# Layer norm statistics of the scan and FFN stage on ScalarE and GpSimd instead of VectorE

## The reference

```
def _layernorm(x, axis=-1, eps=1e-05):
    m = jnp.mean(x, axis=axis, keepdims=True)
    v = jnp.var(x, axis=axis, keepdims=True)
    return (x - m) / jnp.sqrt(v + eps)

x = x + ffn(_layernorm(x))      # x = fwht(x * SU_ug); silu(x @ Wg.T) * (x @ Wu.T); fwht; x @ Wd.T
x = x + ssm(ctx, _layernorm(x)) # the second argument is the gate z:
    state = state * exp(d_t * A) + (d_t * u_t) * B_t ; y_t = state . C_t
    y = (y + D * u) * silu(z)
```

## Time and profile before

| what | value |
|---|---|
| median of three runs | 2714.7 us |
| the profiled execution, its own time | 2715.96 us |
| its span | 2714.2 us |
| granted TensorE clock, mean | 0.917 |
| busy over the span: PE, DVE, POOL, ACT | 85%, 69%, 50%, 45% |
| scan, L1862 DVE, 256 times | mean 1222 ns |
| product, L1873 DVE, 180 times; sum, L1879 DVE, 60 times | mean 691 ns |
| inner, L1887 DVE; add_y, L1893 DVE, 64 times each | mean 750 and 683 ns |
| decay, L1693 ACT, 256 times | mean 692 ns |

### The profile page before, as it was taken

The page is one execution under the profiler, slowest core; times in us unless marked ns, Lnnn a source line. Parts: engine busy times, 40 slices in busy tenths (PEclk is TensorE's granted clock), DMA queues, the critical chain, the costliest instruction groups (busy, mean ns, idle before and its releaser), DMA issues. The chain is left out here.

```text
span 2714.2 us, 35174 instructions
## 1 busy us (share of the span) xinstructions
PE 2294.5 (85%) x10784; PEld 1768.1 (65%) x10785; DVE 1860.2 (69%) x3465; ACT 1229.2 (45%) x2129; POOL 1350.1 (50%) x1083
## 2 busy tenths in 40 slices
PE   3799999999999999997856997998988749468980
PEld 2688888888888888885525665665655427356770
DVE  6476777777676767765757999999989766312223
ACT  2354445445444545443655655656555312123430
POOL 0233333333333333331756778988888602577324
PEclk7799999999999999998977999999999958779995
DMA  7522232221223232112467564654554220755317
GB/s 280 218 75 79 86 110 86 109 87 72 82 86 110 86 110 85 63 67 81 139 219 216 177 205 144 213 175 172 180 195 156 61 90 16 250 164 183 120 54 259
DMA packets 136907, 363.57 MB, mean 134 GB/s; under 512 B 21281, under 2 KB 58913, under 8 KB 118561
## 3 DMA queue, kind: packets, MB, share of 16 engines
q1 hardware_dynamic: 123648, 328.36, 35.6%
q0 software_dynamic: 6320, 20.71, 2.4%
q10 hardware_dynamic: 6768, 12.32, 1.2%
HBM read 290.06 MB, written 71.30 MB: 133 GB/s over the span
## 5 line engine op out<-in xcount | busy, mean ns | idle before, releaser
L664 POOL TENSOR_SCALAR att_probs<-att_probs,att_recip 128x512 f32<-128x512 f32 x256 | 181.7, 713 | 563.1 <-DVE att_recip L731 563.1
L1809 POOL TENSOR_TENSOR mix_drive<-mix_du,mix_rows 128x512 f32<-128x512 f32 x256 | 326.6, 1282 | 63.2 <-DMA mix_rows<-bc_d 28.9
L588 ACT ACTIVATE att_probs<-att_s,att_bias,att_rq 128x512 f32<-128x512 f32 x256 | 200.4, 783 | 289.7 <-DVE att_bias L727 289.6
L1862 DVE TENSOR_TENSOR_SCAN mix_state<-mix_state,mix_drive 128x512 f32<-128x512 f32 x256 | 312.8, 1222 | 15.5 <-POOL mix_drive L1809 10.5
L1693 ACT ACTIVATE mix_state<-mix_delta,mix_a 128x512 f32<-128x512 f32 x256 | 176.7, 692 | 276.9 <-DVE mix_drive L1873 237.7
L1794 POOL TENSOR_TENSOR mix_y<-mix_y,mix_drive 128x512 f32<-128x512 f32 x180 | 230.4, 1280 | 78.2 <-DVE mix_drive L1873 78.2
L1602 PE MATMUL mix_down<-mix_wd,mix_hT 128*128 128x512 f32 x512 | 233.9, 600 | 7.5 <-DVE residual_x L1893 7.5
L726 DVE TENSOR_REDUCE att_nmax<-att_s 128x1 f32<-128x512 f32 x256 | 175.2, 684 | 71.7 <-PE att_s L101 64.8
L767 DVE TENSOR_TENSOR att_pT<-att_pt,att_pT 128x512 fp32r<-128x512 f32 x256 | 170.1, 686 | 65.0 <-ACT att_pT L594 61.3
L594 ACT CAST att_pT<-att_pt 128x512 fp32r<-128x512 f32 x256 | 144.0, 592 | 132.8 <-PE att_pt L445 128.5
L99 PE MATMUL att_w<-att_w_qkv,att_cx 128*128 128x256 f32 x512 | 158.6, 310 | 34.2 <-DVE att_w_qkv L713 25.5
(11 more groups left out here) (348 smaller groups left out, 6718.4 us busy)
## 6 DMA issues: line engine op xcount, KB each, us to landing
att_xn<-normT SPq DMA_DIRECT2D x32, 2048.0 KB
mix_gu<-guT SPq DMA_DIRECT2D x64, 1024.0 KB
mix_rows<-bc_d SPq DMA_DIRECT2D x128, 256.0 KB, 5.0
guT<-att_ffnT SPq DMA_DIRECT2D x32, 512.0 KB, 5.7
mix_wd<-wdT SPq DMA_DIRECT2D x16, 1024.0 KB
slots<-exp_y ACTq DMA_DIRECT2D x47, 256.0 KB
normT<-nrm_outT SPq DMA_DIRECT2D x4, 2048.0 KB, 9.3
exp_raw<-in_L_ffn_Wg SPq DMA_DIRECT2D x16, 512.0 KB
```

Of the source, the lines that this page charges most:

```text
L588: act.activation(probs[:, n, :], ps_s[n % 2][:, :], ACT.Exp, bias=bias[:, n:n + 1], scale=rq[:, n:n + 1], accum_out=sums[:, n:n + 1]).then ...
L664: pool.tensor_scalar(probs[:, n, :], probs[:, n, :], recip[:, n:n + 1], 1.0, ALU.mult, ALU.mult).then_inc(s_pn, 1)
L1809: pool.tensor_tensor(drive[q % RING][:, :], du[i % DUS][:, :], rows[g % ROWS][:, 0, :], ALU.mult).then_inc(s_drive, 1)
L1862: dve.tensor_tensor_scan(h[:, :], h[:, :], drive[q % RING][:, :], 0.0, ALU.mult, ALU.add).then_inc(s_scan, 1)
```

## The change

The statistics leave DVE. For each row tile ACT now runs an Identity pass with an accumulated sum, a multiplication by -1/512 on 128x1, and a Square pass with minus the mean as bias and an accumulated sum (`moments`). `stats(b, j)` does this for one or two row tiles at the end of ACT's steps j = 0 to 3; the passes write their elementwise output into `normT`, which is not read then. Three semaphores make each of the three kinds wait for the one before. POOL makes `rstd` with a power of -0.5 and `shift` (`spread`), three small instructions in its step j = 5, behind its first product there. DVE's list loses `normal_stats`, `gate_stats` and `spread`, and nothing is added to it. In the tail ACT takes the last four row tiles one by one as they are summed, POOL does `spread` behind the last `skip_add`, and the gate follows.

```diff
+                summed, centred, squared = Steps(act, s_sums), Steps(act, s_minus), Steps(act, s_squares)
+
+                def moments(tiles):
+                    squared.wait()
+                    for c, row in tiles:
+                        summed.mark(act.activation(normT[:, c // TB, :], xs[:, row, :], ACT.Identity,
+                                                   accum_out=sums[:, c:c + 1]))
+                    summed.wait()
+                    for c, row in tiles:
+                        centred.mark(act.mul(minus[:, c:c + 1], sums[:, c:c + 1], -1.0 / DIM))
+                    centred.wait()
+                    for c, row in tiles:
+                        squared.mark(act.activation(normT[:, c // TB, :], xs[:, row, :], ACT.Square, bias=minus[:, c:c + 1],
+                                                    accum_out=squares[:, c:c + 1]))
+
+                def stats(b, t):
+                    tiles = []
+                    if b + 1 < B:
+                        tiles.append((t, (b + 1) * TB + t))
+                    if b:
+                        act.wait_ge(s_yadd, BLOCKS * (b - 1) + (CHUNK - 1) * TB + t + 1)
+                        tiles.append((TB + t, (b - 1) * TB + t))
+                        if t == 0:
+                            act.wait_ge(s_rot, KD * min(b, B - 1))
+                    moments(tiles)
 ...
@@ -1759,6 +1786,10 @@
                     if s + 1 < ALL:
                         decay(q + 2)
                         decay(q + 3)
+                    if j < TB:
+                        stats(b, j)
+                    if j == TB:
+                        squared.wait()
 ...
                 for t in range(TB):
+                    stats(B, t)
+                for t in range(TB):
                     z(B - 1, t)
 ...
+                def spread(b, done):
+                    c = slice(0 if b + 1 < B else TB, 2 * TB if b else TB)
+                    if b and b + 1 < B:
+                        pool.wait_ge(s_nrm, TB * b)
+                    if b >= 2:
+                        pool.wait_ge(s_z, TB * (b - 1))
+                    pool.wait_ge(s_squares, done)
+                    pool.tensor_scalar(var_eps[:, c], squares[:, c], 1.0 / DIM, LN_EPS, ALU.mult, ALU.add).then_inc(s_var, 1)
+                    pool.wait_ge(s_var, b + 1)
+                    pool.tensor_tensor(rstd[:, c], var_eps[:, c], power[:, c], ALU.pow).then_inc(s_root, 1)
+                    pool.wait_ge(s_root, b + 1)
+                    pool.tensor_tensor(shift[:, c], minus[:, c], rstd[:, c], ALU.mult).then_inc(s_rs, 1)
+
+                def moments_made(b):
+                    return TB * (b + 1) + TB * b - (TB if b >= B - 1 else 0) - (TB if b == B else 0)
+
+                pool.memset(power[:, :], -0.5).then_inc(s_power, 1)
                 for q in range(RING):
                     force(q)
                 pool.wait_ge(s_const, 64)
+                pool.wait_ge(s_power, 1)
                 for s in range(ALL):
                     b, j = divmod(s, BLOCKS)
                     for q in range(ET * (s + 1), ET * (s + 2)):
                         add(q - RING)
                         if s + 1 < ALL:
                             force(q)
+                        if j == TB + 1 and q % ET == 0:
+                            spread(b, moments_made(b))
 ...
                     skip_add(B - 1, t)
+                spread(B, moments_made(B))
 ...
-                def normal_stats(b, t):
-                    own.mark(dve.bn_stats(stats[:, t, :], xs[:, b * TB + t, :]))
-
-                def gate_stats(b, t):
-                    dve.wait_ge(s_yadd, BLOCKS * b + (CHUNK - 1) * TB + t + 1)
-                    own.mark(dve.bn_stats(stats[:, TB + t, :], xs[:, b * TB + t, :]))
-
-                def spread(first, last):
-                    c = slice(first, last)
-                    own.wait()
-                    for t in range(first, last):
-                        own.mark(dve.bn_aggr(meanvar[:, t, :], stats[:, t, :]))
-                    own.wait()
-                    own.after(dve.tensor_scalar(var_eps[:, c], meanvar[:, c, 1], LN_EPS, None, ALU.add))
-                    newton_rsqrt(dve, own, rstd[:, c], var_eps[:, c], guess[:, c], newton[:, c])
-                    dve.scalar_tensor_tensor(shift[:, c], meanvar[:, c, 0], -1.0, rstd[:, c], ALU.mult,
-                                             ALU.mult).then_inc(s_rs, 1)
-
                 def rotated_lo(b, o):
                     dve.wait_ge(s_rhi, KD * (b - 1) + o + 1)
                     dve.scalar_tensor_tensor(uT[b % 2][:, 1, o, :], spare[o % 2][:, :], SC,
@@ -1945,17 +1979,6 @@
                     if s + 1 < ALL:
                         scan(q + 1)
                         scan(q + 2)
-                    if j < TB:
-                        if b + 1 < B:
-                            normal_stats(b + 1, j)
-                        if b:
-                            gate_stats(b - 1, j)
-                    if j == TB:
-                        if b and b + 1 < B:
-                            dve.wait_ge(s_nrm, TB * b)
-                        if b >= 2:
-                            dve.wait_ge(s_z, TB * (b - 1))
-                        spread(0 if b + 1 < B else TB, 2 * TB if b else TB)
                     if b + 1 < B:
                         if j == 8:
                             rotated_lo(b + 1, 0)
@@ -1976,9 +1999,6 @@
                         scan(q + 3)
                 for n in range(ALL - LAG - 1, ALL):
                     add_y(n)
-                    gate_stats(B - 1, n % TB)
-                dve.wait_ge(s_z, TB * (B - 1))
-                spread(TB, 2 * TB)
                 for t in range(ET):
                     gated(B - 1, t)
                 for t in range(TB):
```

More of the change, by code:

```diff
@@ L1436, in stage_mix @@
         d = m.sb("skip", [P, ET])
[L1437 to L1438 removed]
+        sums = m.sb("sums", [P, 2 * TB])
+        minus = m.sb("minus_mean", [P, 2 * TB])
+        squares = m.sb("squares", [P, 2 * TB])
         var_eps = m.sb("var_eps", [P, 2 * TB])
[L1440 to L1441 removed]
+        power = m.sb("power", [P, 2 * TB])
         rstd = m.sb("rstd", [P, 2 * TB])
```

8 lines of the change are left out of this document (2 added, 6 removed).

## The result

The changed kernel took 2683.44 us (median of 4 runs, 2679.82 to 2687.01), the kernel before 2713.65 (median of 4, 2711.42 to 2715.6): ratio 0.9889, 95% interval 0.9873 to 0.9905. 2695 was predicted, with a range from 2686 to 2712. The direction was right. The profiled execution took 2687.01, its span is 2685.1.

What follows compares the result with a forecast made beforehand. DVE was taken as full, setting the ordinary step at 9.77 us, with POOL next. Terms 2.4 + 6.0 + 8.8 + 5.8 - 1.3 - 0.1 = 21.6 off 2715.96 gave 2694.4, rounded up to 2695; range 2686 to 2712.

Steps and rivals of the forecast that it cites:

- Batch 0, j = 0 to 3: First four steps of batch 0: without the statistic DVE needs 9.16 a step instead of 9.76, 2.4 us saved.
- Batch 0, j = 4: Batch 0's spread step: POOL's spread and ACT's passes are covered, the step falls to 9.76, 6.0 us saved.
- Batches 1 and 2, j = 0 to 3: Steps with two statistics: POOL's unbroken list keeps them at 11.7 each, so nothing is saved.
- Batches 1 and 2, j = 4: Spread steps: ACT's norm waits for POOL, inner comes at 1681.6 instead of 1686.04, 4.4 us saved twice, 8.8.
- Batch 3: Nothing at j = 0 to 3; 8.3 saved at j = 4, of which 1.5 and 1.0 come back: 5.8 us.
- PE: Before the rotations: with less pause from DVE's spreads PE comes later, 1.3 us lost, bounds nothing and 3.7.
- the rival that PE takes the gain back: Each batch's gain at j = 4 only moves the wait to the rotations, some 20 us go: 2713, 7%.
- The tail: After the last add_y: ACT takes 2.1 and POOL 2.4, ending at 2166.5 instead of 2166.39, 0.1 us lost.
- ACT's block: ACT's new statistics work between two decays: 2.1 us for one row tile, 4.1 for two, upper bound 4.6.
- the slower rival: Long hand-overs make ACT's two-tile work 7.6 us: 2725, slower than before from about 6.7, 9%.
- POOL's spread: Inverse root and shift on POOL: power 1.73, two small instructions 0.3 each, 2.4 us in all, bounds 1.8 and 5.3.
- the first rival: POOL's small instructions are dear, the spread takes up to 5.3, each us paid five times: gain 7, 2709, 17%.

Runs made afterwards that it cites:

- the repeat: The changed kernel timed and profiled once more with nothing altered: 2687.05 us, ratio 0.9897 to the kernel before.
- skip_half: Changed kernel with skip_add divided, multiplication on DVE and addition on POOL, and u loads issued earlier: 2675.44 us, ratio 0.9859 to the kernel before.
- half_split: skip_half with ACT's new work cut in two around the fourth decay of a step: 2675.62 us, ratio 0.9843 to the kernel before.

## Why the prediction was wrong

By its steps, with the first profile and the repeat:

- **Batch 0, j = 0 to 3:** 2.4 predicted, 2.39 measured, steps of 9.17. Right.
- **Batch 0, j = 4:** 6.0 predicted, 5.69 and 6.01. Right.
- **Batches 1 and 2, j = 0 to 3:** nothing predicted, 3.2 and 3.7 measured. This is the step that failed. What held is that POOL sets these steps: without the late loads they are equal to 0.1 us with and without the statistics, and they fall when POOL is relieved. What failed is the sentence that POOL "works through" from 1624.52 to 1674.18 and that, nothing being removed from its list, the product comes no earlier. The earlier trace rows has only the two ends of that list. Inside it lie waits for the loads of u, 3.9 us with batch 3, which I had not looked for, and these depend on DVE's steps by way of SyncE's queue. With the statistics gone 0.5 or nothing is left of them.
- **Batches 1 and 2, j = 4:** 8.8 predicted, 9.15 and 9.10. `norm` waits for POOL as described. The step is 13.5 where 13.6 was said.
- **Batch 3:** 5.8 predicted, 6.86 and 6.88. 8.0 came at j = 4 and 0.2 ahead of it, and 1.3 went back in the rest where 2.5 was booked.
- **PE:** a loss of 1.3 predicted. In the first profile the rest of batch 0 is 1.2 longer, in the repeat 0.3 shorter: it is 115.1 in four profiles with the whole change in them and 113.7 in five (in skip_half and half_split j = 15 has new work of its own). What decides between the two is open. The rests of batches 1 and 2 are shorter by 0.3 together. So the term was a loss of 0.9 in the first profile and a gain of 0.5 in the repeat. DVE's waits for PE's down product in the steps are 11.9 and 10.4 where they were 11.1, and the rival that PE takes the gain back is out.
- **The tail:** a loss of 0.1 predicted, 0.8 gained. ACT's block for one tile is 1.8 there and POOL's spread on 128x4 is 1.6, where 2.1 and 2.4 were put.
- **ACT's block:** 4.1 predicted, 3.1 measured. The 7.3 of the path around it was right to 0.05. The error cost nothing in the sum, since POOL's list lay above both, but the cover was 0.8 to 0.9 a step (11.2 against 10.36) and not 0.3, and the even point of the slower rival is 7.1 and not 6.7.
- **POOL's spread:** 2.4 predicted, 2.2 from 1671.88 to the next sum at 1674.07. Its small instructions took 0.20, so the first rival is out, and each us of the spread is paid nearly five times, as was said. The Trainium skill (SBUF — State Buffer, "SBUF: two separate sides") names a DVE instruction with two SBUF inputs or in a two-port mode as one that takes the shared port pair. DVE's scans and products have one input in PSUM, and the 0.20 of POOL beside them agree.

The stage sum is thus 27.2 or 29.4 where 21.6 stood: 3.3 to 3.9 from the loads, 0.9 from the tail, 0.9 from batch 3 besides its load, and the remainder of 0.5 to 2.1 mostly from PE's term. The medians say 30.2, which the stage of the first profile alone does not explain. That the other 1 to 3 us are run-to-run variation outside the stage follows from the repeat (ratio 0.9897) only within its interval of 0.15%. One step of the working had its sign wrong: the prediction rounded up because the profiled execution was 1.3 above the median. That speaks for rounding down: from the median the sum gives 2714.7 - 21.6 = 2693.1, not 2695. With the 3.3 to 3.9 of the loads that would have been some 2689 to 2690, inside the range.

## What to carry over

An engine's list of rows without idle time has to be looked through for small waits before it is called fixed: here 3.9 us of POOL's waits for loads hung on DVE, the very engine that was relieved, through a queue in which the load stood behind another's wait. A load belongs in the queue ahead of what waits longer. When one engine is relieved, compute the next bounds in order (here 9.77 DVE, 10.37 ACT, 11.2 POOL) and take work from the highest; the same move of work from POOL to DVE was worth 7 us after the change and nothing before it. Compare stages step by step: most single steps repeat to 0.05 us, while the time of the unchanged rest moved by 10.

## What was not expected of the hardware

- An ACT pass of 128x512 with an accumulated sum takes 0.61 to 0.72, its accumulator read 0.19, but the two overlap by 0.1 and the next pass follows at 0.61: two row tiles, ten instructions, in 3.1 us.
- A DVE instruction whose tile operands and result are all in SBUF waits out the pass that POOL has in work: the same instruction takes 0.74 with POOL idle and 1.48 when it starts 0.35 into a pass of 1.27, and the multiplication of skip_half takes 0.48 alone, 0.99 with 0.71 of POOL's pass left and 1.22 with 0.94 left. In all of these the duration is what is left of the pass plus the time alone, less 0.2. POOL waits in its turn: its next pass takes 1.72 and not 1.28. Scans and products of DVE, with one operand in PSUM, keep their means of 1.22 and 0.69 in the same steps. The Trainium skill (SBUF — State Buffer, "SBUF: two separate sides") says that a DVE instruction with two SBUF inputs, as the fused one is, or in a two-port mode and one of POOL exclude each other for their whole length; these rows agree. Whether the multiplication, with one tile from SBUF, runs in such a mode no row shows.
- The old spread had paid for it too. Two instructions of one kind and size in the kernel before, the first beside POOL's passes, the second after POOL's last one had ended at 1679.33:

```profile
1676.82 1.19 DVE L113 TENSOR_TENSOR mix_newton<-mix_newton,mix_var_eps 128x8 f32<-128x8 f32 x1
...
1679.59 0.17 DVE L113 TENSOR_TENSOR mix_newton<-mix_newton,mix_var_eps 128x8 f32<-128x8 f32 x1
```

Five of the small instructions of this spread took 0.56 to 1.19, each ending 0.03 after a pass of POOL, and those after 1679.33 took 0.17: some 4.3 of its 8.2 us are such waits, an estimate from these rows. The 0.16 of the earlier trace rows, which the prediction set beside the 1.19 of the earlier trace rows, is of 128x4 and not of the same size. No run took this wait alone out of the old spread.
- Moving sums and products from DVE to ACT, against which the Trainium skill speaks (ScalarE: Activation LUTs, "Rules for kernel authors", which gives `add` and `mul` to VectorE), cost ACT 1.55 for a row tile that cost DVE 0.60, and still paid, because ACT's path of 7.26 lay 3.9 below the 11.2 of those steps, and the two-tile block of 3.1 fitted into that.
